# Layer 3's expert network: rows sorted by chosen expert into blocks of 256, in place of every expert for every row

## What is computed

```python
rh = relu(features @ router_w1 + router_b1)            # 256 -> 128
expert_logits = softmax(rh @ router_w2 + router_b2)    # 6 experts
top_w, top_i = top_k(expert_logits, 2)
routing_weights = softmax(top_w)
h1 = relu(einsum('bsd,edh->bseh', features, expert_w1) + expert_b1)
h2 = relu(einsum('bseh,ehf->bsef', h1, expert_w2) + expert_b2)
expert_out = einsum('bsef,efo->bseo', h2, expert_w3) + expert_b3
combined = sum(take(expert_out, top_i) * routing_weights)
x = x + combined                                       # features = layernorm(x)
```

## Time and profile before

| what | value |
|---|---|
| median of 3 runs | 6234.28 us (6229.06 to 6240.42) |
| profiled execution | 6226.66 us |
| its span | 6224.9 us |
| PE busy | 4421.3 us, 71% |
| DVE busy | 3114.8 us, 50% |
| ACT busy | 2093.4 us, 34% |
| POOL busy | 1604.5 us, 26% |
| mean granted TensorE clock | 0.86 of full |
| read from and written to HBM | 542.72 MB, 118.31 MB |

### The profile page before, as it was taken

The page is one execution under the profiler, slowest core; times in us unless marked ns, Lnnn a source line. Parts: engine busy times, 40 slices in busy tenths (PEclk is TensorE's granted clock), DMA queues, the critical chain, the costliest instruction groups (busy, mean ns, idle before and its releaser), DMA issues. The chain is left out here.

```text
span 6224.9 us, 60406 instructions
## 1 busy us (share of the span) xinstructions
PE 4421.3 (71%) x18528; PEld 2913.3 (47%) x18528; DVE 3114.8 (50%) x5879; ACT 2093.4 (34%) x3991; POOL 1604.5 (26%) x1751
## 2 busy tenths in 40 slices
PE   1230046995574777969996798996794958797898
PEld 1230034775110565757775223223673636574676
DVE  8432035112796538841215998985884035444211
ACT  5100001212484104622222787884552110203222
POOL 1466665665575531100000211100111020000000
PEclk9965578997687888979998898997896989898899
DMA  9400045116344435520001444441552227361000
GB/s 383 165 1 1 0 132 164 35 39 175 118 158 133 147 120 203 176 57 0 0 0 56 149 151 138 156 143 59 202 169 92 87 74 240 97 197 31 1 0 21
DMA packets 405631, 664.32 MB, mean 107 GB/s; under 512 B 108992, under 2 KB 210360, under 8 KB 399864
## 3 DMA queue, kind: packets, MB, share of 16 engines
q1 hardware_dynamic: 368152, 654.14, 31.8%
q0 software_dynamic: 37216, 7.08, 0.7%
HBM read 542.72 MB, written 118.31 MB: 106 GB/s over the span
## 5 line engine op out<-in xcount | busy, mean ns | idle before, releaser
L1205 PE MATMUL l2g_a_agg_acc<-all_x,l2g_a_h 128*65 128x512 f32 (+1 forms) x1400 | 646.6, 587 | 23.9 <-ACT l2g_a_agg_flat L1230 21.1
L394 POOL DMA_INDIRECT far<-all_nil,all_far_cell x416 | 495.2, 1190 | 299.3 <-DMA far<-all_nil,all_far_cell 147.2
L394 POOL DMA_INDIRECT table<-first_count,first_cell x416 | 405.8, 975 | 409.1 <-issue 279.6
L1303 DVE SCALAR_TENSOR_TENSOR all_x<-all_x,l2g_a_agg_counts 128x512 f32<-128x512 f32 (+1 forms) x700 | 404.6, 625 | 119.0 <-ACT all_x L1253 118.3
L862 PE MATMUL l0g_agg_acc<-l0g_agg_halves,l0g_agg_exact 128*128 128x512 f32 x625 | 153.5, 400 | 338.1 <-DVE l0g_agg_exact L915 334.2
L1242 ACT ACTIVATE l2g_a_agg_z<-l2g_a_agg_z 128x512 f32<-128x512 f32 (+1 forms) x700 | 344.4, 538 | 143.4 <-PE l2g_a_agg_z L1185 119.0
L862 PE MATMUL l3g_agg_acc<-l3g_agg_halves,l3g_agg_exact 128*128 128x512 f32 x1250 | 303.7, 397 | 92.5 <-DVE l3g_agg_exact L915 87.5
L1253 ACT ACTIVATE all_x<-l2g_a_agg_z 128x512 f32<-128x512 f32 (+1 forms) x700 | 353.7, 569 | 0.1
L1797 DVE SCALAR_TENSOR_TENSOR all_x<-l1f_moe_py,l1f_gate,all_x 128x256 f32 x200 | 96.7, 484 | 439.9 <-PE l1f_moe_py L1754 439.9
L862 PEld LDWEIGHTS l3g_agg_acc<-l3g_agg_halves,l3g_agg_exact 128*128 128x128 f32 x1250 | 236.9, 191 | 155.1 <-DVE l3g_agg_exact L915 88.2
L394 POOL DMA_INDIRECT table<-all_count,all_cell x256 | 263.1, 1028 | 169.3 <-DMA table<-all_count,all_cell 78.7
(11 more groups left out here) (759 smaller groups left out, 9305.1 us busy)
## 6 DMA issues: line engine op xcount, KB each, us to landing
l3g_agg_counts<-table SPq DMA_DIRECT2D x250, 320.0 KB
l2g_a_agg_counts<-table SPq DMA_DIRECT2D x300, 256.0 KB
table<-counting_eye_rows SPq DMA_DIRECT2D x25, 1600.0 KB, 38.3
l0g_agg_counts<-table SPq DMA_DIRECT2D x125, 320.0 KB
l1g_agg_counts<-table SPq DMA_DIRECT2D x125, 320.0 KB
l2g_a_agg_mask<-far SPq DMA_DIRECT2D x50, 800.0 KB
l1g_gat_agg_counts<-table SPq DMA_DIRECT2D x150, 256.0 KB
l2g_b_agg_counts<-table SPq DMA_DIRECT2D x150, 256.0 KB
```

The lines of the kernel that those rows point to most:

```text
L394: pool.indirect_dma_start(self.table, bass.IndirectOffsetOnAxis(ap=self.cell[:, b, p:p + 1], axis=0), self.count(b, p), None, bounds_check ...
L1205: pe.matmul(to, rhs(t, r * per + h), p[:, u % n_p, 0:n], start=(t == 0), stop=(t == nt - 1), skip_group_check=True).then_inc(summed, 1)
L1303: dve.scalar_tensor_tensor(out=w, in0=w, scalar=1.0, in1=counts[:, b % n_counts, 0:n], op0=ALU.min, op1=ALU.mult).then_inc(weighted, 1)
```

## The change

Layer 3's expert part computes only the chosen experts. A row of the new buffer `few_in` in DRAM is WIDE = 260 floats long: the 256 features, and two pairs of (target row, gate), one pair per choice. The buffer has 2 x 18 blocks of 256 rows: 18 for the first choices, 18 for the second, each half sorted by expert, each expert rounded up to whole blocks. 18 is a bound that holds for any routing, so that all 36 blocks are always computed, and an unused place holds zeros and a target row of 1e6, which the scatter's bounds check drops.

- `layernorm` gets `blank`: POOL clears a tile of 9 x 260 floats per partition, and SP then writes it 8 times over `few_in` (9.6 MB). The loads of the expert weights there are gone, and with them `settle`.
- `top2_gates` is replaced by `top2_places`: choices, places, the expert of each block (`owner`), gates and target rows into columns 256 to 259 of the normalised rows.
- `experts` is replaced by `top2_experts`. POOL scatters the 25 tiles to the first half, waits for them, and scatters them to the second half. SP fetches for each block its three matrices, biases and rows; the expert comes from a register loaded from `owner`. Weights and rows have RING = 5 buffers. DVE scales a block's results by the gates, POOL scatters them to `few_out` (HELD = 8 buffers).
- When all are there, SP reads both halves of `few_out` back, DVE adds them to x, and SP writes the output by groups. The stage `end` is gone.

The diff, cut to its core:

```diff
+NOBODY = 1e6
+BLOCK = 2 * P
+WIDE = D + 4
+RING, HELD = 5, 8
...
+            if blank is not None:
+                tile, nobody, places = blank
+                @block.gpsimd
+                def _(pool):
+                    pool.memset(tile, 0.0).then_inc(blank_set, 1)
...
+                @block.sync
+                def _(sp):
+                    sp.wait_ge(blank_set, 2)
+                    for place in places:
+                        sp.dma_start(place, tile).then_inc(c.loaded[0], 16)
...
-            top2_gates(nc, "l3f_top", c, score, ne, gate)
-        settle(nc, "l3f_settle1", c, 1)
-        experts(nc, "l3f_moe", c, xt, x, gate, ne, ...)
+            top2_places(nc, "l3f_top", score, ne, per, xn, put, owner)
+        top2_experts(nc, "l3f_moe", c, a, x, xn, put, owner, per, out)
...
+def top2_places(nc, tag, score, ne, per, xn, put, owner):
...
+                first_max(dve, link, score, ne, prio, top, one[:, :, 0, :], tmp)
...
+                first_max(dve, link, score, ne, prio, top_b, one[:, :, 1, :], tmp)
+                dve.sem_inc(chosen, 1)
...
+                dve.wait_ge(summed, 1)
+                link(dve.tensor_copy(pos[...], pp[:, 1, 0:T * n2]))
+                for t in range(T):
+                    link(dve.tensor_tensor(tot[:, t + 1, :], tot[:, t, :], pos[:, t]..., ALU.add))
...
+def top2_experts(nc, tag, c, a, x, xn, put, owner, per, out):
...
+            @block.sync
+            def _(sp):
+                for i in range(nb):
+                    k = i % RING
+                    if i >= RING:
+                        sp.wait_ge(res_ready, i - RING + 1)
+                    e = sp.value_load(owner[0:1, i:i + 1], min_val=0, max_val=5)
+                    for j in range(3):
+                        sp.dma_start(w[:, k, j], a[f + f"expert_w{j + 1}"][ds(e, 1)]...).then_inc(w_in[k], 16)
...
+                        for j in range(2):
+                            sp.dma_start(b[:, k, j], a[f + f"expert_b{j + 1}"][ds(e, 1), :]...).then_inc(w_in[k], 16)
+                    sp.dma_start(b3[:, k], a[f + "expert_b3"][ds(e, 1), :].to_broadcast([P, D])).then_inc(w_in[k], 16)
+                    if i % per == 0:
+                        sp.wait_ge(put_done, i // per + 1)
+                    sp.dma_start(rows[:, k], c.few_in[i * BLOCK:(i + 1) * BLOCK, :]...).then_inc(rows_in[k], 16)
+                sp.wait_ge(all_put, 1)
+                for g in range(T // G1):
+                    for i in range(2):
+                        sp.dma_start(y[:, i, g * G1:(g + 1) * G1, :], c.few_out[...]).then_inc(y_in[g], 16)
+                for g in range(T // G1):
+                    sp.wait_ge(x_ready, 2 * (g + 1))
...
+                    sp.dma_start(out[...], x[:, g * G1:g * G1 + n, :]).then_inc(out_in, 16)
...
+            @block.gpsimd
+            def _(pool):
+                pool.wait_ge(c.loaded[0], c.n_loaded[0])
+                for i in range(2):
+                    for t in range(T):
+                        pool.indirect_dma_start(c.few_in, ...put[:, t, i:i + 1]..., xn[:, t, :], ...)
+                    pool.wait_ge(c.few_landed[i], 16 * T)
+                    pool.sem_inc(put_done, 1)
+                for i in range(nb):
+                    pool.wait_ge(res_ready, i + 1)
+                    for t in range(rt):
+                        pool.indirect_dma_start(c.few_out, ...ids[:, i % HELD, t:t + 1]..., res[:, i % HELD, t, :], ...)
...
+            @block.tensor
+            def _(pe):
+                for i in range(nb + 3):
+                    if i < nb:
+                        pe.wait_ge(rows_in[i % RING], 16 * (i // RING + 1))
...
+                    j = i - 1
...
+                    j = i - 2
...
+                    j = i - 3
...
+            @block.vector
+            def _(dve):
+                for i in range(nb + 3):
+                    if i < nb:
...
+                    j = i - 3
+                    if j >= 0:
...
+                        dve.wait_ge(y_ps, j + 1)
...
+                        dve.tensor_tensor(res[:, j % HELD], py[:, j % 2], over_mid(b3[:, j % RING], rt), ALU.add)
+                        dve.tensor_copy(ids[:, j % HELD, :], rows[:, j % RING, :, D + 2 * choice])
...
+                        for t in range(rt):
+                            last = dve.tensor_scalar(res[:, j % HELD, t, :], ..., None, ALU.mult)
+                        last.then_inc(res_ready, 1)
```

More of the change, by code:

```diff
@@ L591, in _, with layernorm @@
                     dve.tensor_reduce(degree[:, 0:nt], part[:], AX, ALU.add).then_inc(summed, 1)
-def layernorm(nc, tag, c, x, xn, fm=None, unit=False, ahead=(), beside=None):
+def layernorm(nc, tag, c, x, xn, fm=None, unit=False, ahead=(), beside=None, blank=None):
     with Scope(nc, tag) as s:
@@ L605, in layernorm @@
         pt = s.ps("pt", [P, 4, KD, 2 * P])
-        with stage(nc, tag, "stat", "agg", "eps", "root", "step", "done", "turned", "out") as (
-                block, stat, agg, eps, root, step, done, turned, out):
+        with stage(nc, tag, "stat", "agg", "eps", "root", "step", "done", "turned", "out", "blank_set") as (
+                block, stat, agg, eps, root, step, done, turned, out, blank_set):
             if beside is not None:
@@ L2129, in build @@
         small_landed = top.cx.enter_context(nc.semaphore("small_landed"))
+        per3 = (NP + 6 * (BLOCK - 1)) // BLOCK
+        c.few_in = nc.dram_tensor("few_in", (2 * per3 * BLOCK, WIDE), F32, kind="Internal").ap()
+        c.few_out = nc.dram_tensor("few_out", (2 * NP, D), F32, kind="Internal").ap()
+        c.few_landed = [top.cx.enter_context(nc.semaphore(f"few{i}_landed")) for i in range(2)]
+        c.res_landed = [top.cx.enter_context(nc.semaphore(f"res{i}_landed")) for i in range(HELD)]
         c.put_landed = top.cx.enter_context(nc.semaphore("put_landed"))
@@ L2300, in build @@
             part(nc, c, a, x, (table1, far1, table2, far2), dinv, (scatter2, scatter_far))
[L2302 to L2307, removed]
+        l3_ffn(nc, c, a, x, (table1, far1, table2, far2), dinv, (scatter2, scatter_far), out)
 def l0_gnn_start(nc, c, x, xt, w, gw, h, z, degree, dinv, scatter, at):
@@ L2891, in _, with l3_ffn @@
                         dve.tensor_copy(nm[:, t, :], pt[:, t % 8, 0:D]).then_inc(out, 1)
-def l3_ffn(nc, c, a, x, tables, dinv, scatters):
+def l3_ffn(nc, c, a, x, tables, dinv, scatters, out):
     ne = 6
+    per = (NP + ne * (BLOCK - 1)) // BLOCK
     f = "L3_ffn_"
     with Scope(nc, "l3f") as s:
[L2898 to L2902, removed]
+        xn = s.sb("xn", [P, T, WIDE])
+        put = s.sb("put", [P, T, 2], U32)
+        owner = s.sb("owner", [P, 2 * per], I32)
         with Scope(nc, "l3fr") as q:
+            xt = q.sb("xt", [P, KD, NP])
             w1, b1, w2, br = c.small.l3f_w1, c.small.l3f_b1, c.small.l3f_w2, c.small.l3f_b2
@@ L2906, in l3_ffn @@
             score = q.sb("score", [P, T, ne])
[L2907 to L2911, removed]
+            blank = q.sb("blank", [P, 9, WIDE])
+            every = c.few_in.rearrange("(p r) d -> p r d", p=P)
+            layernorm(nc, "l3f_ln", c, x, xn[:, :, 0:D], xt, blank=(
+                blank[:], blank[:, :, D:WIDE], [every[:, r:r + 9, :] for r in range(0, 2 * per * BLOCK // P, 9)]))
             product_fm(nc, "l3f_r1", [xt[:, k] for k in range(KD)], w1, rh, ACT.Relu, b1)
```

216 lines of the change are left out of this document (214 added, 2 removed).

## The result

The changed kernel took 6215.89 us (median of 10 runs, 6201.39 to 6217.23) against 6233.51 us for the kernel before (10 runs, 6219.15 to 6240.42): a ratio of 0.9969, 95% interval 0.9960 to 0.9978. It is faster, by 0.31%; the forecast was 1.2%, or 73 us. The profiled execution took 6217.09 us on a span of 6215.4.

What follows compares the result with a forecast made beforehand. PE bounds the old stage, computing 19,200 row-expert pairs; the change computes 9,216. Terms: +46.7 ahead of the experts, -142 blocks, +22 end, -73 on a span of 6224.9: 6152, or 6161 on the median's scale; range 6075 to 6225.

Steps and rivals of the forecast that it cites:

- Clearing: Ahead of the experts: SP's 8 writes of 9.6 MB delay the places stage's end by 0 to 6 us, taken as 3.
- Places: Ahead of the experts: computing places, scaled from layer 2's 13.6 us, takes 20.7 us and ends at 5786.6.
- Scatter to pass 0: From last place to PE's first transpose: first choice's 25 indirect DMAs, landing and row load, 39.1 us as in layer 2.
- Start-up: Passes 0 to 4, without the ring's wait, filling up: 18 us, with the second choice's scatter lying beside them.
- The loop: Passes 5 to 35 at 8.3 us each, 257 us, PE waiting for rows because slots free late.
- D: In the loop, time from SP's wake-up to landed rows: 8.1 us, bounds 6 and 11.
- DVE's tail: In the loop, DVE's work after a pass ends, before the slot is free: 1.6 us.
- The end: After the last third-layer matmul: scatters, reading results, adding, output take 37.4 us against 15.5 before, +22.
- The ring hides it: Rival for the loop: D under 4 or loads further ahead, PE bounds at 5.8 per pass, 6083; chance 0.22.
- The clock falls in every pass: Rival for the loop: PE's clock drops every pass, twice in some, 9.5 per pass, 6198; chance 0.14.
- SP's chain: Slower rival for the loop: a block's transfers run one after another, D 19 us, 13.2 per pass, 6313; chance 0.10.
- The page's rule: Loads of 256 KB: a fixed 2.0 us per DMA, paid seven times per block, would make the change lose; trace says hidden.

Runs made afterwards that it cites:

- scatter spread: Changed kernel with the second choice's scatter cut in nine pieces of three, each ahead of the wait for a result of blocks 1 to 9: 6192.0 us.
- spaced: Changed kernel with a fill on POOL after each of the second choice's 25 scatters, leaving gaps between them: 6194.1 us.
- the thin one: Changed kernel whose second scatter moves only 4 of 260 columns per row into an unread array, leaving the second choice's part out of the output: 6205.5 us.
- the best version: "four edits" with only blocks 0 to 4's weights issued ahead, and the second scatter in single pieces after early passes, then one or two per result: 6070.8 us.
- rows-first: Changed kernel with SP issuing each block's rows ahead of its weights and biases, block 0 excepted: 6110.7 us.
- four edits: Changed kernel with seven slots, rows ahead of weights, seven blocks' weights before the scatter wait, second scatter in twos, first-choice results added during last passes: 6088.6 us.
- weights first: Changed kernel with weights and biases of blocks 0 to 4 issued before SP waits for the first scatter, their rows right after: 6198.0 us.

## Why the prediction came out as it did

The sign was right and 6215.9 lies in the range (6075 to 6225), which says little, as the range reached up to 9 us below the kernel before. The time was forecast 55 us too low, and of the 73 us of gain 17.6 came. By its steps:

- **Clearing** (+3 forecast, nothing measured). From layernorm to router it is 21.9 us in both kernels. SP had issued the eight writes by 5737.4, in 8.22 us, 11 us before the router began.
- **Places** (20.7 forecast): 19.8, from POOL's first constant at 5774.1 to the last DVE instruction at 5793.9. The steps scaled from the earlier trace rows held.
- **Scatter to pass 0** (39.1 forecast): 37.5, to 5831.39. The earlier trace rows was the right model, and wider rows cost nothing. The three together make the -5.5.
- **Start-up, the step that failed** (18 forecast, 61.3 measured). "The second choice's scatter ... lies beside the first blocks" was costed at POOL's own time, as if it used only POOL and the DMA engines. Runs with the scatter spread or spaced take 28 us off, the thin one shows that it is the issuing. The trace of before had a steady scatter, but with all other engines waiting for it, so it could not show what it does to them. I asked what queues behind it on POOL, and not what else it runs beside. The other 15 us are the sum's own: 0.5 + 2.2 + 4.0 + 5.7 + 5.7 leaves out that SP's issuing of one block began 3.8 to 5.2 us behind that of the block before in these two runs, and that pass 5 already waits for the ring (10.7 and 10.2 us for pass 4 in these two runs, as the chain has it). With all that out of the way, in the best version, it is 19.8.
- **The loop** (8.3 per pass forecast, 8.87 measured). The mechanism, the pairs, the one who waits and whom for, D (8.3 for 8.1) and DVE's tail were right. So was the clock as one low stretch per pair: 17.2 to 17.3 us a pair is the 8.6 that stood beside it, and the 8.3 taken "between the first two" was below what the trace of before supported. That is 9 to 10 us of the 17. Most of the rest is three pairs that took longer. In two of them, at 5900 and 6058 us (20.2 and 20.0 us), SP issued its matrices in 2.4 to 2.5 us in place of 1.40, as here:

```profile
6060.41 2.39 SPq L3076 DMA_DIRECT2D l3f_moe_w<-in_L_ffn_expert_w  x3
```

In the trace a transfer of 16 KB of instructions begins at both places (5902.76 and 6060.94). That it is the cause was not tried. In the third, at 6130 us (19.2), the stalled pass was 0.6 us longer, and in the next PE's low clock reached into one more layer (2.76 us in place of 1.89). With seven slots the issuing has such cases too (2.84 us at 5870.89), and no pass of the loop is longer for it.
- **The end** (37.4 forecast from the last third-layer matmul): 38.9, by the route that was forecast. The four last scatters of results stood in a row on POOL and cost some 1 us more than the two of the sum. Then the data were last: the loads came at 350 GB/s, and DVE began each group's additions when its data landed, one group per 3.76 us, of which it worked 3.02.

```profile
6183.06 13.75 SPq L3090 DMA_DIRECT2D l3f_moe_y<-few_out  x10
...
6189.55 3.02 DVE L3210 TENSOR_TENSOR all_x<-all_x,l3f_moe_y 128x1280 f32<-128x1280 f32 x2 [11.56 <-DMA l3f_moe_y<-few_out]
...
6204.52 3.02 DVE L3210 TENSOR_TENSOR all_x<-all_x,l3f_moe_y 128x1280 f32<-128x1280 f32 x2 [0.66 <-DMA l3f_moe_y<-few_out]
```

```profile
6193.00:6198.00 5.00, 0.00 (x0) 0.00 (x0) 3.90 (x3) 0.00 (x0) 0.00 (x0) 0.50 1.10 348
```

"The DVE additions lie beside the reading but for the last two, which the earlier groups' output covers" held: while the last two ran, the DMA engines still moved 379 GB/s (5 us from 6203). With half of the reading and adding done earlier the last stretch is 10 us shorter; half of 6.55 MB at 350 GB/s is 9.4 us.
- **The rivals.** "The ring hides it" was far off for five slots (20 waits, 16 of them from pass 5 on), but it is what six slots give. "The clock falls in every pass" is the picture of four slots (0.70). SP's chain bounds nothing at 3.5 to 4 us a block, but it is the term that rows-first cuts.
- **The page's rule** (at least 1 MiB per DMA, the Trainium skill, "DMA: Bandwidth & Descriptors"). The page gives the prediction's 2.0 us for DMAs that GpSimd issues, and these are SP's. With seven slots the same 256 KB loads run at 242 GB/s through the loop, with their seven landings hidden, and the 5.6 us of a pass show no fixed part. With five slots a landing is on the chain in every second pass. So the weighing held: the fixed part counts where someone waits, and here the order of issue decided who did.

## What to carry to other kernels

Count a ring's slots from the step that frees one to the step that needs it: if the pipeline itself lags three passes, five slots leave two, and one pass of work, result, issue and landing (here 5.6 + 1.6 + 8.3 = 15.5 us) must fit into two passes of work (11.2). With six slots they have three passes (16.9), and fit. Issue first what is needed first; here this, or one more slot, was worth some six times the whole gain of the change. And a long run of indirect DMAs that POOL issues back to back may not be free for its neighbours: look at what the other engines do beside it, and if they are held back, put work or waits between the DMAs, or cut the run into pieces so small that they don't join up with POOL's other DMAs.

## What the chip showed that was not expected

While POOL issued the second choice's scatters without a pause, SP's instructions, its register moves too, took 0.70 us each or were held for multiples of it, and ACT and DVE began 3.7 to 7.0 us after their operands were ready; beside twelve scatters in a row in "four edits" single matmuls of PE came 1.42 us apart. With rows of 16 bytes it is the same, with one scatter per 2.3 us it isn't there. But scatters in a row are not enough for it. Under the second scatter in one piece it began with the first, second or third instruction, where SP had anything to issue by then. Under the first scatter, as long and as steady, the first step came after 6 us in "four edits" and after 9 in "weights first", a steady row of them after 16 and 14, and in "best", which issues the same five blocks there as "weights first", there were none. And in the version with gaps POOL afterwards issued twelve scatters of results in a row, from 5888.51 to 5903.6, beside which SP issued two blocks in its usual times:

```profile
5888.51 0.97 POOL L3118 DMA_INDIRECT few_out<-l3f_moe_res,l3f_moe_ids  x1 [2.57 <-DMA few_in<-l3f_xn,l3f_put]
...
5896.39 1.42 SPq L3076 DMA_DIRECT2D l3f_moe_w<-in_L_ffn_expert_w  x3
```

What else must come together, and which part of the chip is short here, no run shows. Gaps and short pieces are what was tested, and not the longest run that would go unpunished.
